# A kernel of four blocks on one core: order of the first block's queues, and who issues the first loads

## The reference

```
qkv     = x @ Wqkv                        (per head: q, k, v of 16 channels)
scores  = q @ k.T / (sqrt(16) * 0.72) * alpha, shifted per row by its maximum
weights = softmax(scores)
x       = layernorm(x + gate(x) * (weights @ v) @ Wproj + bproj)
```

## Time and profile before

| | us |
|---|---|
| median of 3 runs | 2671.85 |
| lowest, highest | 2671.34, 2677.64 |
| profiled execution | 2680.05 |
| its span (first to last instruction) | 2678.1 |
| TensorE, VectorE, ScalarE, GpSimd busy | 2404.8, 1640.3, 1235.1, 713.7 |

### The profile page before, as it was taken

The page is one execution under the profiler, slowest core; times in us unless marked ns, Lnnn a source line. Parts: engine busy times, 40 slices in busy tenths (PEclk is TensorE's granted clock), DMA queues, the critical chain, the costliest instruction groups (busy, mean ns, idle before and its releaser), DMA issues.

```text
span 2678.1 us, 39615 instructions
## 1 busy us (share of the span) xinstructions
PE 2404.8 (90%) x14896; PEld 1401.3 (52%) x14896; DVE 1640.3 (61%) x4283; ACT 1235.1 (46%) x2758; POOL 713.7 (27%) x707
## 2 busy tenths in 40 slices
PE   4789998999879889887689999999999999999996
PEld 1223333333354267666355666666666666666664
DVE  5656667667451055665676667666676677676653
ACT  0455555455421134111366566565556655565530
POOL 1121223231011032111433333323332333333310
PEclk7789999999999989998899999999999999999998
DMA  8132333232413912000000000000000100000001
GB/s 280 39 102 75 105 104 114 81 103 82 145 71 131 421 79 80 17 17 17 26 5 5 2 5 5 5 5 2 28 13 12 42 10 19 5 21 21 19 21 33
DMA packets 70941, 158.38 MB, mean 59 GB/s; under 512 B 6320, under 2 KB 48416, under 8 KB 63168
## 3 DMA queue, kind: packets, MB, share of 16 engines
q1 hardware_dynamic: 68448, 146.68, 15.8%
q0 software_dynamic: 2304, 9.18, 1.5%
HBM read 116.52 MB, written 35.13 MB: 57 GB/s over the span
## 4 chain that ended last, share of the span: by engine, by line
PE 70%; DVE 13%; DMA 6%; ACT 3%; issue 3%; POOL 3%; SPq 1%; POOLq 0%; DVEq 0%; ACTq 0%
PE banks L1788 8%; PE banks L1766 6%; PE banks L1663 6%; PE banks L1675 4%; PE banks L245 4%; PE banks L221 4%; PE banks L213 3%; PE banks L1737 3%; PE banks L1706 3%; PE banks L1748 3%; DMA arena<-stacks 2%; PE banks L1294 2%; PE banks L1721 2%; PE banks L265 2%; DVE arena L2257 2%
## 5 line engine op out<-in xcount | busy, mean ns | idle before, releaser
L449 DVE TENSOR_REDUCE arena<-banks 128x1 f32<-128x512 f32 x512 | 318.1, 682 | 118.9 <-PE banks L213 118.8
L353 ACT ACTIVATE arena<-banks 128x512 f32<-128x512 f32 x512 | 279.4, 595 | 141.6 <-PE banks L221 139.6
L1788 PE MATMUL banks<-arena 128*128 128x512 f32 x640 | 293.3, 594 | 6.1 <-DVE arena L1993 6.1
L1859 ACT ACTIVATE arena<-arena 128x256 f32<-128x256 f32 (+1 forms) x512 | 286.3, 562 | 2.5 <-DVE arena L1957 2.1
L2060 POOL TENSOR_TENSOR arena<-arena 128x512 f32<-128x512 f32 x128 | 162.6, 1271 | 445.1 <-DVE arena L1977 445.1
L213 PE MATMUL banks<-arena 96*128 96x512 bf16 x512 | 207.0, 407 | 56.0 <-DMA arena<-stacks 37.8
L1663 PE MATMUL banks<-arena 128*128 128x512 f32 x512 | 246.9, 606 | 5.0 <-DVE arena L1977 4.2
L1951 DVE CUSTOM_DVE_ANT_0 arena<-banks,arena 128x256 f32<-128x256 f32 (+1 forms) x512 | 169.2, 386 | 83.1 <-PE banks L1706 83.0
L221 PE MATMUL banks<-arena 128*128 128x512 bf16 x512 | 201.5, 396 | 15.6 <-ACT arena L353 10.4
L1788 PEld LDWEIGHTS banks<-arena 128*128 128x128 f32 x640 | 117.7, 190 | 138.3 <-issue 126.9
L2056 POOL TENSOR_TENSOR arena<-arena 128x16 f32<-128x16 f32 x64 | 187.5, 2930 | 5.4
(11 more groups left out here) (290 smaller groups left out, 4374.3 us busy)
## 6 DMA issues: line engine op xcount, KB each, us to landing
arena<-in_e_W SPq DMA_DIRECT2D x32, 1024.0 KB, 12.4
arena<-stacks SPq DMA_DIRECT2D x64, 384.0 KB, 4.4
arena<-in_e_Wg SPq DMA_DIRECT2D x16, 1024.0 KB, 14.7
stacks<-arena SPq DMA_DIRECT2D x32, 384.0 KB, 2.6
stacks<-arena SPq DMA_DIRECT2D x32, 256.0 KB, 3.1
arena<-dens POOLq DMA_DIRECT2D x32, 256.0 KB, 4.6
arena<-in_xT SPq DMA_DIRECT2D x8, 512.0 KB, 10.6
arena<-in_x SPq DMA_DIRECT2D x8, 512.0 KB, 9.9
```

The costliest lines, as they stand in the source:

```text
L353: e.activation(ex[:, j], self.psum[:, 3 + k % 2], ACT.Exp).then_inc(s["a_e"], 1)
L449: e.tensor_reduce(mx[:, t, j:j + 1], self.psum[:, k % 3], AX.X, ALU.max, negate=True).then_inc(s["a_m"], 1)
L1788: i = e.matmul(bank, weights[:, c], self.hT[:, c], start=c == 0, stop=c == 1)
L1859: k = e.activation(pr[:, h, at:], pr[:, h, at:], ACT.Exp, bias=mx[:, h:h + 1], scale=rn[:, h:h + 1], accum_out=den[:, h:h + 1])
```

## The change

1. The key side of a half is computed at t = 1 instead of t = 2 of the same unit.
2. TensorE does the values matmuls of the step before between the second and the third pair of a step, not behind the fourth.
3. In SyncE's loop the step's stores stand ahead of `fetch1` of unit u+3. At the start they are ordered by half: q and k of half 0, fetch of units 0 and 1, q and k of half 1, fetch of units 2 and 3.
4. The first two halves' q and k are computed ahead of the first sequence's v. VectorE's setup is put into a function of its own and stands between the cuts of half 0 and those of half 1.
5. SyncE loads only sequence 0's transposed input, the qkv weights and a small group of constants. ScalarE waits for these weights and then issues the other twenty loads, ahead of everything else that it does. The natural inputs get semaphores n0 to n7 of their own, and counts on x0 to x7 fall by 16. The constants that the setup reads move to the group that is loaded first.

```diff
-                    at[4 * k + 2 * h, 2 * side].append(("qk", 2 * k + 2 + h, side))
+                    at[4 * k + 2 * h, side].append(("qk", 2 * k + 2 + h, side))
...
-EARLY1 = [("qk", 0, 0), ("qk", 0, 1), ("v", 0, 0), ("v", 0, 1), ("v", 0, 2), ("v", 0, 3), ("qk", 1, 0), ("qk", 1, 1)]
+EARLY1 = [("qk", 0, 0), ("qk", 0, 1), ("qk", 1, 0), ("qk", 1, 1), ("v", 0, 0), ("v", 0, 1), ("v", 0, 2), ("v", 0, 3)]
...
-            if before is not None:
-                self.tensor1_values(e, w, *before)
+                if j == 1 and before is not None:
+                    self.tensor1_values(e, w, *before)
...
@@ tensor1_gate
+        w.wait_ge("l_small", 16)
...
@@ vector1
         w.wait_ge("l_keep", 16)
-        w.wait_ge("l_small", 16)
...
-        for task in EARLY1:
+        for task in EARLY1[:2]:
+            self.vector1_task(e, w, *task)
+        self.vector1_setup(e, w)
+        for task in EARLY1[2:]:
             self.vector1_task(e, w, *task)
...
@@ sync1
-        for task in EARLY1:
-            self.sync1_task(e, w, *task)
-        for u in range(4):
-            self.fetch1(e, w, u)
+        for unit in range(2):
+            self.sync1_task(e, w, "qk", unit, 0)
+            self.sync1_task(e, w, "qk", unit, 1)
+            self.fetch1(e, w, 2 * unit)
+            self.fetch1(e, w, 2 * unit + 1)
...
+            for task in self.at1[u, t]:
+                self.sync1_task(e, w, *task)
             if t == 1 and u >= 1 and u + 3 < UNITS:
                 self.fetch1(e, w, u + 3)
-            for task in self.at1[u, t]:
-                self.sync1_task(e, w, *task)
...
@@ fetch1
-        w.wait_ge("a_made_v", 8)
...
@@ scalar
+        self.loads(e, w)
         self.scalar1(e, w)
...
@@ sync
+        e.dma_start(self.xT[:, 0, :, 1:], xT[:, 0]).then_inc(s["x0"], 16)
+        e.dma_start(self.w1qkv, split(d["a_wqkv"], CHUNKS, 3, CH)).then_inc(s["l_wqkv"], 16)
         e.dma_start(self.pieces["keep"], d["keep"]).then_inc(s["l_keep"], 16)
...
+    def loads(self, e, w):
+
+        s, d = self.s, self.dram
+        xT = split(d["xT"], SEQS, CHUNKS, TOKENS)
+        w.wait_ge("l_wqkv", 16)
+        e.dma_start(self.pieces["small"], d["small"]).then_inc(s["l_small"], 16)
+        for b in range(1, SEQS):
+            e.dma_start(self.xT[:, b, :, 1:], xT[:, b]).then_inc(s["x%d" % b], 16)
+        e.dma_start(self.wqk, split(d["a_wqk"], CHUNKS, H1, 2 * HD1)).then_inc(s["l_wqk"], 16)
+        for b in range(SEQS):
+            e.dma_start(self.x_nat[:, b], d["x"][b].rearrange("(t p) c -> p t c", p=P)).then_inc(s["n%d" % b], 16)
+            if b == 0:
+                e.dma_start(self.w1proj, split(d["a_wproj"], 4, CH)).then_inc(s["l_wproj"], 16)
+        for n, name in enumerate(("d_Wq", "d_WkT")):
+            e.dma_start(self.slot_w[n], split(d[name], CHUNKS, CH)).then_inc(s["l_slot"], 16)
...
-        group = "keep" if n == "identity" else "late" if n[:4] in ("b_10", "b_11", "b_20", "b_21", "l_g0", "l_g1", "l_b0", "l_b1", "wind") else "small"
+        group = "keep" if n in ("identity", "a_alpha", "a_beta", "ones5") else "late" if n[:4] in ("b_10", "b_11", "b_20", "b_21", "l_g0", "l_g1", "l_b0", "l_b1", "wind") else "small"
```

More of the change, by code:

```diff
@@ L262, in tensor1_task @@
             w.wait_ge("l_wqkv", 16)
-            w.wait_ge("x%d" % b, 32)
+            w.wait_ge("x%d" % b, 16)
             for k in range(CHUNKS):
@@ L267, in tensor1_task @@
         elif kind == "v":
-            w.wait_ge("x%d" % unit, 32)
+            w.wait_ge("x%d" % unit, 16)
             for k in range(CHUNKS):
@@ L415, in vector1 @@
         w.wait_ge("l_keep", 16)
-        w.wait_ge("l_small", 16)
+        e.tensor_scalar(self.alpha, S("a_alpha"), HD1 ** -0.5 / 0.72, None, ALU.mult).then_inc(s["a_setup"], 1)
         e.tensor_copy(self.ident16, self.ident).then_inc(own.up(), 1)
[L418 to L438, removed]
-        for task in EARLY1:
+        for task in EARLY1[:2]:
+            self.vector1_task(e, w, *task)
+        self.vector1_setup(e, w)
+        for task in EARLY1[2:]:
             self.vector1_task(e, w, *task)
@@ L462, in vector1, with vector1_setup @@
                 self.vector1_task(e, w, kind, unit, index)
+    def vector1_setup(self, e, w):
+        s, S, own = self.s, self.S, self.own1
+        beta, rest = self.beta16, self.brest
+        e.tensor_copy(beta[:, 0], S("a_beta")).then_inc(own.up(), 1)
+        w.wait_ge(own.sem, own.n)
+        e.tensor_tensor(rest[:, 0], S("a_beta"), beta[:, 0], ALU.subtract).then_inc(own.up(), 1)
+        w.wait_ge(own.sem, own.n)
+        e.tensor_copy(beta[:, 1], rest[:, 0]).then_inc(own.up(), 1)
+        w.wait_ge(own.sem, own.n)
+        e.tensor_tensor(rest[:, 1], rest[:, 0], beta[:, 1], ALU.subtract).then_inc(own.up(), 1)
+        w.wait_ge(own.sem, own.n)
+        e.tensor_copy(beta[:, 2], rest[:, 1]).then_inc(own.up(), 1)
+        for n in range(4):
+            stack = self.stack[n]
+            e.memset(stack[STACK:P, 0:UNIT * TOKENS // 2], 0.0).then_inc(s["a_made_v"], 1)
+            e.tensor_copy(split(stack.bitcast(BF16), 2, UNIT * TOKENS)[STACK:P, 1],
+                          S("ones5")[STACK:P].to_broadcast([P - STACK, UNIT * TOKENS])).then_inc(s["a_made_v"], 1)
+        w.wait_ge(own.sem, own.n)
+        w.wait_ge("a_made_p", 6)
+        for g in range(4):
+            for n in range(3):
+                e.tensor_copy(self.shift16[g][:, :, 2 + n], repeated(beta[:, n, 4 * g:4 * g + 4], TILES)).then_inc(own.up(), 1)
     def vector1_aside(self, e, w, u):
@@ L608, in gpsimd1_task @@
         elif kind == "v" and index == 0:
-            w.wait_ge("x%d" % unit, 32)
+            w.wait_ge("n%d" % unit, 16)
             w.wait_ge("l_small", 16)
@@ L1916, in vector4 @@
                 if d < LAYER:
-                    w.wait_ge("x%d" % (d // TILES), 48)
+                    w.wait_ge("x%d" % (d // TILES), 32)
                 e.tensor_tensor(x, x, self.psum[:, 2, 0:CH], ALU.add).then_inc(self.s["t_x"], 1)
@@ L2016, in vector4_mlp @@
                     w.wait_ge("m_xw", 2 * m + 2)
-                    w.wait_ge("x%d" % b, 64)
+                    w.wait_ge("x%d" % b, 48)
                     e.tensor_tensor(x, x, split(self.again, TILES, CH), ALU.add).then_inc(s["f_add"], 1)
@@ L2128, in sync4 @@
                 w.wait_ge("f_add", b)
-            w.wait_ge("x%d" % b, 48)
+            w.wait_ge("x%d" % b, 32)
             e.dma_start(self.again, self.kept_dram[b]).then_inc(s["x%d" % b], 16)
@@ L2135, in sync4 @@
         for b in range(SEQS):
-            w.wait_ge("x%d" % b, 80)
+            w.wait_ge("x%d" % b, 64)
     def shift4(self, e, w, m):
@@ L2154 @@
 class Program(Block1, Block2, Block3, Block4):
-    SEMS = ["l_keep", "l_small", "l_late", "l_wqkv", "l_wproj", "l_wqk", "edge"] + ["x%d" % b for b in range(SEQS)]
+    SEMS = ["l_keep", "l_small", "l_late", "l_wqkv", "l_wproj", "l_wqk", "edge"] + [n % b for n in ("x%d", "n%d") for b in range(SEQS)]
     COLUMNS = 206 * 256 + 448
@@ L2183, in layout @@
         self.xT = split(r.take(SEQS * CHUNKS * (TOKENS + 1)), SEQS, CHUNKS, TOKENS + 1)
-        self.small_from = r.at + 128 + 64 + 64
-        self.pieces = {"keep": r.take(128)}
+        self.pieces = {"keep": r.take(self.dram["keep"].shape[-1])}
         self.half, self.ident16 = r.take(64), r.take(64).bitcast(BF16)
+        self.small_from = r.at
         self.pieces["small"] = r.take(self.dram["small"].shape[-1])
```

## The result

The changed kernel is slower: median 2721.19 us of 4 runs (2713.86 to 2723.99), beside 2674.74 us of 4 runs of the kernel before. The ratio is 1.017, with a 95% interval of 1.0144 to 1.0196. That is +46 us, 1.7%, where +40 was forecast.

What follows compares the result with a forecast made beforehand. The prediction took TensorE's queue, busy 90% of the span, as the bound, with no slack at 12 fetch waits. Its terms, +51 + 14 - 26 + 0.6 = +40 us, gave a median of 2712 us, range 2666 to 2745.

Steps and rivals of the forecast that it cites:

- Term 1, the fetch: SyncE's queue at (u,1), u even: fetch u+3 waits behind key-side stores, 4.1 us for each of 12: +51 us.
- The gather, costed at nothing: GpSimd's gather, queued behind the second cut, comes 7.6 us later but falls into TensorE's same stall: no cost.
- Term 2, the clock: TensorE after the new stalls: runs at 1.2 GHz for a while, 1.5 us at 9 places: +14 us.
- Term 3, the values: TensorE's steps: values matmuls fill waits for exponential banks (92 steps, 0.22 each) and for VectorE: -26 us.
- Term 4, the start: Kernel start: ScalarE's loads hold it until about 28 us, first maximum about as before: +0.6 us, nothing gained.
- Absorbed late fetches: Rival at SyncE's fetches: late fetches cost nothing, first two terms vanish, kernel ends faster at 2646; chance 0.12.
- the free issue of ScalarE's queue: Rival at the start: ScalarE's issue is not held, the start gains 13 us, 2699; chance 0.18.
- The late gather: Rival: VectorE, blocked at the reciprocal, lets maxima slip 3 us for six sequences, slow clock doubles: 2744; chance 0.12.

Runs made afterwards that it cites:

- e11: Kernel before with only fetch u+3 of even units moved behind the key side's stores at (u,2): 2783.07 us, ratio 1.0405.
- e1: Changed kernel with fetch u+3 again issued ahead of the step's stores, key side still at t = 1: 2661.09 us, ratio 0.9966.
- e2: Changed kernel with the key side back at t = 2, values, start and loads as changed: 2639.62 us, ratio 0.9884.
- e3: Kernel before with only the values matmuls moved between the second and third pair: 2638.41 us, ratio 0.9879.
- e4: Kernel before with only the new start (loads on ScalarE's queue, first task order, VectorE's setup between cuts): 2673.88 us, ratio 1.0.
- e7: e2 with ScalarE's first evictions put ahead of its loads of natural inputs and last weights: 2619.74 us, ratio 0.9796.
- e6: e3 with fetch u+3 of even units issued at t = 0, ahead of everything else: 2632.93 us, ratio 0.9849.

## Why the prediction was right

- *Term 1, the fetch.* Predicted +51, measured +49.5 (44.6 in the window from 180 us and 4.9 at u = 2, where 2 was put in). Its instants held too. For u = 10 it put the issue 3.4 us later and the landing 4.2: counted from the query side's cut they came 3.2 and 4.0 later. That no slack covers a later fetch is shown by e11, where the same cause stands alone, and by e1, where undoing it takes 60 us away. The extra 0.8 us behind the stores was about right: from issue to use 5.85 us here, 5.0 before.
- *The gather, costed at nothing.* Right for this kernel, and right in its reason: it falls into the same stall of TensorE. But it is a second cause of that stall. It appears once the first is taken away, at 21 us (e1 against e2; the prediction had said up to 30). That the two chains end within 0.2 us of each other was not foreseen.
- *Term 2, the clock.* The mechanism held, since every fetch wait of 4 us and more has a window at 1.2 GHz behind it. Its size is not settled. The windows of the steady part give half-clock time as 2 x (1 - clock) x length: 79 us instead of 31, so up to 24 us of TensorE's time instead of 14. But that is an upper bound: in e11 the same sum gives 137 us instead of 31 (clock 0.89 over 622.9 us), up to 53 us, and only 17 were left beyond the waits.
- *Term 3, the values.* This term is mis-sized. Alone they are worth 34 us (e3), not 26. An ordinary step gains 0.36 us (4.93 to 4.57), not 0.22. Steps at t = 1 gain little: (9,1), with its shift rows, takes 3.30 us before and 3.27 in e3. Two things outside the term take part as well: in e3 the fetch waits grew from 17.3 to 27.0 us, because TensorE arrives earlier, and the clock of the steady part rose from 0.97 to 0.99. How much of this gain the changed kernel keeps isn't measured. The prediction said that 36 of the 128 steps only feed a stall, and e2 bears on it: e2 has the whole gain and only two fetch waits over 2.4 us, and 76 to 82 us lie between it and the changed kernel where terms 1 and 2 gave 65. The clock could account for that gap as well.
- *Term 4, the start.* +0.6 predicted, +3.8 at the first maximum, about +2 in the time and not told from zero (e4). The mis-sized step is how long ScalarE is held: until 32 us instead of 28. The rule of the Trainium skill, page DMA: Bandwidth & Descriptors, section "Issuing engines are not separate DMA queues", that a second issuer saves only the time to initiate, "usually small", did not give the -13 that I worked out from it as a rival: issuing twenty loads took ScalarE 25 us, and e7 shows that these, not the transfers, stood ahead of the first eviction.
- *The sum.* The 40 lies near the 46 partly by luck: term 3 was too small a gain and term 2 probably too small a loss, and the two errors work against each other. The 6 us that are missing can't be put down to one of them. The stated range, 2666 to 2745, would also have held a kernel that had not changed at all.
- *Rivals.* Absorbed late fetches and the free issue of ScalarE's queue are refuted by e11 and e7. The late gather did not add: TensorE's waits for VectorE at line 213 are 8.9 us in the changed kernel and 12.8 before.

## What to carry to other kernels

In an engine's queue that issues transfers, a wait belongs to everything behind it: put the transfer that is due next first, and one whose source is still being made last. When two chains end in the same stall, undoing one shows only part of what the pair costs, so undo both. A compute engine that also issues loads should first do the work that others wait for.

## What the runs showed of the hardware

Issuing from a second engine did not make the issues short. ScalarE's first issue took 0.38 us, its seven transposed inputs 5.58 and its last seven natural inputs 12.62, and the 11 MB kept it from 6.6 to 32 us. Split, the first 9 of its issues were over by 13 us, and the rest were issued from 34.5 us on while it had nothing else to do.

Long waits cost more than their length: in e11, 89 us more of them, 6.5 to 10.7 us each, made the kernel 106 us slower. The windows behind them show the granted clock at its lower level, 1.2 GHz. The length of the wait alone doesn't tell which waits do this: in e6 a wait of 2.13 us (at 277.77) was followed by 3.4 us at 1.00, one of 2.14 us (at 566.60) by 3.4 us at 0.53.
